# A decoder layer on one core: another hand-written order of steps where the attention ends and the gated layer begins

## What is computed

```python
def _L0_attn_ref(x_q, w_q, w_k, w_v, w_o):
    q = jnp.einsum('ntc,hdc->nhtd', x_q, w_q)
    k = jnp.einsum('ntc,hdc->nhtd', x_q, w_k)
    v = jnp.einsum('ntc,hdc->nhtd', x_q, w_v)
    a = jnp.einsum('nhtd,nhsd->nhts', q, k) / math.sqrt(q.shape[3])
    a = jnp.where(causal_forbidden[None, None], -jnp.inf, a)
    a = jax.nn.softmax(a, axis=3)
    y = jnp.einsum('nhts,nhsd->nthd', a, v).reshape(a.shape[0], t, -1)
    return y @ w_o
...
def _L0_ffn_ref(x, w1_w, w1_s, w2_w, w2_s, h1_w, h1_s, h2_w, h2_s, w3_w, w3_s):
    h = jax.nn.silu(_tlin(x, w1_w, w1_s)) * _tlin(x, w2_w, w2_s)
    h = jax.nn.gelu(_tlin(h, h1_w, h1_s), approximate=False)
    h = jax.nn.gelu(_tlin(h, h2_w, h2_s), approximate=False)
    return _tlin(h, w3_w, w3_s)
...
x = x + _L0_attn_ref(_layernorm(x, axis=-1), ...)
x = x + _L0_xattn_ref(_layernorm(x, axis=-1), ctx_1024, ctx_1024, mask_SxS2_ik1, ...)
x = x + _L0_ffn_ref(_layernorm(x, axis=-1), ...)
```

## Time and profile before

| | us |
|---|---|
| three runs | 1509.94 to 1510.55, median 1510.31 |
| the profiled execution | 1507.81 |
| its span, first to last instruction | 1506.0 |
| PE busy | 1487.9 (99%) |
| DVE busy | 1101.3 (73%) |
| ACT busy | 968.6 (64%) |
| POOL busy | 492.1 (33%) |

### The profile page before, as it was taken

How to read it: one execution, slowest core, us unless ns; L and a number is a source line. 1 busy time by engine, 2 the same in 40 slices (tenths; PEclk the granted TensorE clock), 3 DMA queues, 4 the chain that set the end, 5 groups by cost and what they waited for, 6 DMA issues and landing times.

```text
span 1506.0 us, 29162 instructions
## 1 busy us (share of the span) xinstructions
PE 1487.9 (99%) x10680; PEld 1262.7 (84%) x10680; DVE 1101.3 (73%) x2772; ACT 968.6 (64%) x2274; POOL 492.1 (33%) x763
## 2 busy tenths in 40 slices
PE   8999999999999999999998999999999999999999
PEld 6888888888888888888887788888888888888887
DVE  7999999999999899999999657555553634444443
ACT  6888888888888888888887754456444532222222
POOL 2545454445544555454453011000110212221110
PEclk9999999999999999999999999999999999999999
DMA  4000000000000000000013423421212632222221
GB/s 155 2 1 2 30 2 30 1 2 30 2 29 1 2 30 1 16 15 2 22 64 113 145 84 113 150 103 66 79 66 78 215 114 85 84 85 84 85 84 43
DMA packets 56024, 87.15 MB, mean 58 GB/s; under 512 B 4416, under 2 KB 33472, under 8 KB 55872
## 3 DMA queue, kind: packets, MB, share of 16 engines
q1 hardware_dynamic: 55872, 85.10, 16.5%
HBM read 55.72 MB, written 29.36 MB: 56 GB/s over the span
## 4 chain that ended last, share of the span: by engine, by line
PE 91%; DVE 5%; ACT 2%; DMA 1%; issue 1%; POOL 0%; SPq 0%; DVEq 0%
PE bank L1024 15%; PE bank L1026 13%; PE bank L658 10%; PE bank L578 9%; PE bank L630 8%; PE bank L580 7%; PE bank L579 7%; PE bank L642 6%; PE bank L1179 2%; PE bank L1170 2%; PE bank L1032 2%; PE bank L1146 2%; PE bank L1138 2%; PE bank L1139 2%; PE bank L1140 2%
## 5 line engine op out<-in xcount | busy, mean ns | idle before, releaser
L844 POOL TENSOR_SCALAR P<-P,stats 128x512 f32<-128x512 f32 (+3 forms) x512 | 269.0, 544 | 376.4 <-DVE stats L822 376.1
L717 ACT ACTIVATE P<-P,stats 128x384 f32<-128x384 f32 (+3 forms) x512 | 283.9, 560 | 16.4 <-DVE stats L814 16.2
L681 ACT ACTIVATE PT<-bank 128x512 fp32r<-128x512 f32 (+1 forms) x384 | 185.4, 525 | 87.6 <-PE bank L642 86.5
L814 DVE CUSTOM_DVE_ANT_0 P<-bank,cmask 128x384 f32<-128x384 f32 (+3 forms) x512 | 228.4, 483 | 1.2 <-PE bank L630 0.9
L731 DVE TENSOR_TENSOR PT<-bank,PT 128x512 fp32r<-128x512 f32 (+1 forms) x384 | 218.8, 594 | 5.3 <-ACT PT L681 4.1
L1336 DVE TENSOR_TENSOR Hb<-gt,Hb 128x512 fp32r<-128x512 f32 x128 | 90.8, 710 | 167.0 <-ACT Hb L1187 165.9
L1024 PE MATMUL bank<-Hb,hw 128*128 128x512 f32 x512 | 202.3, 395 | 0.8 <-DVE Hb L1336 0.8
L1024 PE MATMUL bank<-w,hw 128*128 128x512 f32 x512 | 199.2, 389 | 0.0
L658 PEld LDWEIGHTS bank<-PT,V 128*128 128x128 f32 x1024 | 165.0, 190 | 22.1 <-DVE PT L731 4.3
L658 PE MATMUL bank<-PT,V 128*128 128x512 f32 (+3 forms) x1024 | 176.7, 320 | 3.5 <-DVE PT L731 3.5
L1026 PE MATMUL bank<-Hb,hw 128*128 128x512 f32 x448 | 174.8, 390 | 0.0
(11 more groups left out here) (230 smaller groups left out, 3305.4 us busy)
## 6 DMA issues: line engine op xcount, KB each, us to landing
h_scratch<-go SPq DMA_DIRECT2D x64, 256.0 KB, 2.0
xs<-x_scratch SPq DMA_DIRECT2D x23, 512.0 KB, 4.1
hx<-h_scratch SPq DMA_DIRECT2D x32, 256.0 KB, 6.1
stageA<-in_h SPq DMA_DIRECT2D x14, 512.0 KB, 3.6
x_scratch<-x SPq DMA_DIRECT2D x8, 512.0 KB, 3.0
x_scratch<-xs SPq DMA_DIRECT2D x8, 512.0 KB, 2.9
qf<-h_scratch SPq DMA_DIRECT2D x16, 256.0 KB, 5.3
pf<-h_scratch SPq DMA_DIRECT2D x16, 256.0 KB, 6.0
```

What stands on the lines that cost most here:

```text
L681: return e.activation(dst, src, ACT.Copy, scale=scale)
L717: e.activation(p, p, ACT.Exp, bias=st_[:, k:k + 1], scale=-1.0, accum_out=st_[:, 8 + k:9 + k]).then_inc(s_exp, 1)
L814: e.tensor_tensor_reduce(P_tile(P, i, a), banks["S", P, max(i, 1)][a][:, slice(*S_COLS[i])], cmask[:, 512 - n:512], -1.0, 3.0e38, ALU.add, ...
L844: e.tensor_scalar(p, p, stats[P % 4][:, k:k + 1], 1.0, ALU.mult, ALU.mult).then_inc(s_norm, 1)
```

## The change

Only the tail lists change. The instructions are the same on every engine, in other places, and the line numbers of the new kernel are higher by one from here on.

```diff
-        T.63.1 O.62 xo.0.0 xo.0.1 AV.63.0 AV.63.1 xv.2 xv.3 xt.0.1.0 xt.0.1.1 ft.2 O.63 O.64 g.0.0 u.0.0 g.0.1
-        u.0.1 g.0.2 u.0.2 g.0.3 u.0.3 g.0.4 u.0.4 g.0.5 u.0.5 g.0.6 u.0.6 g.0.7 u.0.7 ft.3""",
+        T.63.1 O.62 xo.0.0 xo.0.1 AV.63.0 AV.63.1 xv.2 xv.3 xt.0.1.0 xt.0.1.1 ft.2 g.0.0 u.0.0 g.0.1 u.0.1 g.0.2
+        u.0.2 O.63 O.64 g.0.3 u.0.3 g.0.4 u.0.4 g.0.5 u.0.5 g.0.6 u.0.6 g.0.7 u.0.7 ft.3""",
...
-        xload.0 st.6 mb ld.0 ld.1 ld.2 ld.3 ld.6 ld.5 ld.4 ld.7 ld.8 ld.9 ld.10 ld.11 ld.13 ld.14 st.7 ld.12
-        ld.15 xload.1 ld.16""",
+        xload.0 st.6 mb ld.0 ld.1 ld.2 ld.3 ld.6 ld.5 ld.4 ld.7 ld.8 ld.9 ld.10 ld.11 ld.13 ld.14 xload.1 st.7
+        ld.12 ld.15 ld.16""",
```

More of the change, by code:

```diff
@@ L144 @@
         e.63.1.1 big.5 e.63.0.0 xvh.0 xcc e.63.0.1 xvh.1 big.6 yo.62.0 xe.0 yo.62.1 ph.63.0.0 ph.63.2.1 xph.0
-        ph.63.0.1 ph.63.1.0 ph.63.1.1 ph.63.2.0 fh.7 fh.8 big.7 yo.63.0 fh.9 yo.63.1 big.8 xvh.2 fh.10 xvh.3
-        xth.0.1.0 xth.0.1.1 big.9 fh.11 big.10 silu.0.0 silu.0.1 big.11 silu.0.2 hh.0.1 silu.0.3 hh.0.3 silu.0.4
-        fh.12 silu.0.5 fh.13 fh.14 big.12 hh.0.5 silu.0.6 silu.0.7 fh.15 hh.0.6 hh.0.7 fh.16 big.13 big.14""",
+        ph.63.0.1 ph.63.1.0 ph.63.1.1 ph.63.2.0 fh.7 fh.8 yo.63.0 yo.63.1 fh.9 big.7 xth.0.1.0 xth.0.1.1 big.8
+        xvh.2 silu.0.0 xvh.3 fh.10 big.9 silu.0.1 fh.11 big.10 silu.0.2 hh.0.1 big.11 silu.0.3 hh.0.3 fh.12
+        silu.0.4 silu.0.5 fh.13 fh.14 big.12 hh.0.5 silu.0.6 silu.0.7 fh.15 hh.0.6 hh.0.7 fh.16 big.13 big.14""",
     "DVE": """
@@ L168 @@
         pl.62.0.0 pl.62.1.1 m.63.0.0 pl.62.0.1 m.63.0.1 fl.6 xvl.0 r.63.0 xs1.0 xs2.0 xs3.0 xs4.0 os.61 ys.62.0
[L169 to L172, removed]
+        xvl.1 xr.0 ys.62.1 pl.63.0.0 pl.63.2.1 xpl.0 pl.63.0.1 pl.63.1.0 pl.63.1.1 pl.63.2.0 os.62 xoa.0.0
+        xoa.0.1 lsum.0.1 fl.7 lnorm.0.1 fl.8 xtl.0.1.0 xtl.0.1.1 xva.2 flag.2 xva.3 fm.2 ys.63.0 ys.63.1 fl.9
+        xvl.2 xvl.3 hm.0.0 hm.0.1 hl.0.0 fl.10 hm.0.2 hl.0.1 fl.11 os.63 os.64 lsum.1.0 hm.0.3 hl.0.2 hl.0.3
+        hm.0.4 fl.12 hl.0.4 hm.0.5 lnorm.1.0 hl.0.5 hm.0.6 flag.3 fm.3 hm.0.7 hl.0.6 hl.0.7 fl.13 fl.14 fl.15
+        fl.16""",
     "POOL": """
@@ L182 @@
         n.62.1.0 n.62.0.0 n.62.1.1 yh.61 yl.61 n.63.2.1 pz n.63.3.1 n.63.3.0 n.63.2.0 n.63.1.1 n.63.0.1 n.63.0.0
-        n.63.1.0 yh.62 yl.62 lpow.0.1 yh.63 yl.63 hh.0.0 hh.0.2 hh.0.4 lpow.1.0""",
+        n.63.1.0 yh.62 yl.62 lpow.0.1 yh.63 yl.63 hh.0.0 hh.0.2 lpow.1.0 hh.0.4""",
     "SP": """
-        xload.0 st.6 mb ld.0 ld.1 ld.2 ld.3 ld.6 ld.5 ld.4 ld.7 ld.8 ld.9 ld.10 ld.11 ld.13 ld.14 st.7 ld.12
-        ld.15 xload.1 ld.16""",
+        xload.0 st.6 mb ld.0 ld.1 ld.2 ld.3 ld.6 ld.5 ld.4 ld.7 ld.8 ld.9 ld.10 ld.11 ld.13 ld.14 xload.1 st.7
+        ld.12 ld.15 ld.16""",
 }
```

## The result

| | before | after |
|---|---|---|
| median | 1509.13 us (1505.20 to 1510.55) | 1515.70 us (1513.83 to 1516.24) |
| profiled execution | 1507.81 us | 1515.51 us |
| its span | 1506.0 us | 1513.7 us |
| mean granted clock of it | 0.999 | 0.995 |

The ratio is 1.0045, with a 95% interval of 1.0031 to 1.0059: the changed kernel is 6.8 us slower (4.7 to 8.9), where +8.2 was forecast; the two profiled executions lie 7.7 us apart. The median of before is 1.2 us lower here than the one that the forecast started from, since later executions were added.

A forecast was written before the change was run, and what follows sets the result against it. PE is 99% busy, so only its waits or clock can move the time. h.0.0 later by 7.9 to 8.0 us, less 1.4, gives +6.6; clock 1.6 makes +8.2: 1518.5 us from median 1510.31, range 1515.0 to 1521.0.

The forecast's parts named there:

- Part 3: From g.0.0 over os.64, store, load and fh.12 to flag.3: PE waits some 10.5 us, h.0.0 starts 7.9 to 8.0 us later.
- four waits: PE's waits before the change, 796 to 850 us: 2.93 before AV.63, 1.47 before xt.0.1, 0.81 before ft.3, 0.22 in g.0.0.
- the 1.4 us that come back: From ft.3 to xt.1.0.0, inside h.0.0: 1.4 us of the delay regained, as the hl and layer norm are nearly done.
- the wait costs its 2.9 us and 1.5 us more: At AV.63 in the kernel before: the wait for the last pl costs 2.9 us, the lowered clock behind it 1.5.
- Part 1: Last low part first: AV.63 starts 2.5 us sooner at full clock, 1.5 more; after the layer norm, xt runs 4.2 us ahead.
- lpow: Layer norm step on POOL, directly behind fl.7 on DVE: taken as 2.4 us, with 1.02 as the other end.
- A second fall of the clock: Between 812 and 817 us, where waits of 1.5 and 2.1 us stand close together: 0 to +0.8 us.
- 1.6 for the clock: At the start of h.0.0, after PE's 10.5 us wait: low clock costs 1.6 us, ends 0 and 1.7.
- if a later stage takes the delay in: Behind the reordered place: one of three stated signs that the forecast is wrong; no size given.

The follow-up runs named there:

- e3: The changed kernel with the third last weight load ahead of the store, two pieces' tiles changed for it: 1513.56 us, ratio 1.0030.
- e4: The changed kernel with the row sums os.63 and os.64 two places sooner on DVE: 1514.42 us, ratio 1.0037.
- e7: The kernel before with PE's new list alone, all other engines in the old order: 1514.55 us, ratio 1.0043.
- e1: The kernel before with the last low part pl.63.2.0 alone moved forward on DVE: 1507.37 us, ratio 1.0000.
- e0: The changed kernel run once more, unedited, against the kernel before: median 1515.8 us, ratio 1.0045.
- e5: The changed kernel with 40 filler products on PE before ft.3: 1515.65 us, ratio 1.0044.

## Why the prediction was right, and where it was not

The forecast said slower, by one mechanism, and the time lay where it said. Point by point:

- **Chain to `flag.3` (Part 3): held.** os.64 ended at 832.4 (831.9 said), PE stood 10.53 us (10.5), and e3 and e4 show by intervention that the store and the row sums are on the path. That fh.12 started at 838.64 (838.6) is in part luck: os.64 was 0.5 us late, and the way from it over store and load took 6.2 us instead of 6.7. ACT stood 2.86 us for the load, not some 4, since hh.0.3 came in between. `big.12` was done at 843.78 as said (843.8), and what made `ft.3` 0.8 us late came behind it: ACT stood 0.38 us for hm.0.5, which was behind hl.0.4 and its 0.51 us for POOL's hh.0.4 (1.52 us long), and hm.0.6 stood on DVE behind the layer norm and hl.0.5 (845.93), steps that the sum of Part 3 left out.
- **"four waits": too few.** Inside h.0.0 before had two more, 0.78 and 0.27 us. The sum has them all the same, as most of the 1.4 us that come back.
- **"the wait costs its 2.9 us and 1.5 us more": wrong for the wait, nearly right for the clock.** The `xt.0.1` of before, e7 and e1, laid side by side, put the wait at nothing and the slow clock at 1.2 us up to there. Part 1 itself had the layer norm as what sets PE's place, and the sum went by the chain of Part 3, so the error had no weight in it.
- **`lpow` (Part 1): mis-sized.** 1.93 us instead of 2.4; it began 0.2 us behind fl.7 and was done at 811.96, 0.9 us behind the end of fl.7. With a layer norm of 1.38 us, `xt.0.1` came at 813.43 instead of 813.9.
- **A second fall of the clock, held as an end of +0.8: happened**, from 816.5 to 819.9 in after, from 818.1 to 821.5 in e0. The first six halves took 7.0 us instead of 6.25, and the ten after the output products ended at 836.2, 0.6 us later than said. The chain of Part 3 began at 819.0 (818.9 said), so it cost next to nothing at the end.
- **The 1.4 us that come back inside h.0.0, and 1.6 for the clock: right.** From `ft.3` to `xt.1.0.0` after took 5.54 us, as before took 5.62; e5, at full clock there, took 3.85. So by this one execution 1.8 came back and the clock took 1.7. `xt.1.0.0` came 8.8 us later where 8.2 were said, by the later `ft.3`.
- **"if a later stage takes the delay in": a part was.** Before, PE waited at 971.78 us for rows that stood on DVE behind a look at a load.

```profile
971.78 0.47 PE L1138 MATMUL bank<-XTs,w 128*128 128x512 f32 x1 [0.45 <-DVE XTs L1336]
```

  After, that product (979.66) has no wait, so of 8.5 us just ahead of it 7.9 are left behind it, and 7.7 at the end. This is read from the two traces; no run tests it. So the difference of 7.7 us near the forecast of 8.2 is again a sum of errors that partly cancel: 0.6 more up to `xt.1.0.0`, and 1.1 less behind it.
- **The median**: +6.8 us by the ratio against +7.7 in the profiled pair and +8.2 forecast. The interval (4.7 to 8.9) holds all three. The forecast time lies 2.8 us above the measured median: 1.2 us of that is its base, the rest the difference (6.6 us between the medians).
